# A four-layer graph network on one core: semaphores cleared inside blocks, scatters shared out anew, and products of constants where TensorE waits

## The reference

```python
edge_index = jnp.stack([src, dst])
x = _layernorm(x + _L0_gnn_ref(x, edge_index, W, b, a, 3125))
x = _layernorm(x + _L1_gnn_ref(x, edge_weight, W_lin, att_l, att_r, W_res, edge_index))
x = _layernorm(x + _L2_gnn_ref(x, edge_index, w_in, b_in, ...))
x = _layernorm(x + _L3_gnn_ref(x, weight, gamma, beta, src, dst, edge_type_8))
# layer 0, per head: num = segment_sum(exp(-lrelu(s_src[src] + s_dst[dst])) * h[dst], src); elu(num / row_sum)
# layer 1, 8 heads: softmax over dst of lrelu(edge_weight * (alpha_l[src] + alpha_r[dst])); sum of x[src]
# layer 2, two rounds: softmax over dst of q[dst].k[src] * scale; sum of v[src]; then w_o and a dense block
# layer 3: agg = segment_sum((h @ weight[rel])[src], dst); batch norm of agg
```

## Time and profile before

| | us |
|---|---|
| median of 3 runs (4961.72 to 4969.9) | 4966.9 |
| profiled execution, its own time | 4954.8 |
| its span, first to last instruction | 4953.0 |
| TensorE busy in the span | 3592.7 (73%) |
| DVE busy | 3404.9 (69%) |
| POOL busy | 2835.4 (57%) |
| ACT busy | 2076.2 (42%) |
| mean granted clock of TensorE | 0.854 of full speed |

### The profile page before, as it was taken

How to read it: one execution, slowest core, us unless ns; L and a number is a source line. 1 busy time by engine, 2 the same in 40 slices (tenths; PEclk the granted TensorE clock), 3 DMA queues, 4 the chain that set the end, 5 groups by cost and what they waited for, 6 DMA issues and landing times. The chain is left out here.

```text
span 4953.0 us, 58113 instructions
## 1 busy us (share of the span) xinstructions
PE 3592.7 (73%) x16423; PEld 2694.9 (54%) x16423; DVE 3404.9 (69%) x6660; ACT 2076.2 (42%) x4216; POOL 2835.4 (57%) x2961
## 2 busy tenths in 40 slices
PE   2455566654997887757888879978888799755553
PEld 1322455541456666634666658856666676444443
DVE  8876788866876666686999985579999642222225
ACT  1047444523873333244666644446666333100001
POOL 2775777757767777403777731057776210277772
PEclk9779777777997887878999989989999899877776
DMA  1100777762005554524888861178888321333334
GB/s 53 35 2 18 188 184 181 184 123 63 2 21 143 138 138 132 88 87 158 239 239 239 235 137 44 37 213 240 239 238 212 106 79 69 120 105 105 105 105 65
DMA packets 294343, 632.59 MB, mean 128 GB/s; under 512 B 70842, under 2 KB 149663, under 8 KB 290847
## 3 DMA queue, kind: packets, MB, share of 16 engines
q0 software_dynamic: 157120, 435.48, 33.7%
q1 hardware_dynamic: 136926, 193.54, 13.0%
HBM read 562.78 MB, written 66.02 MB: 127 GB/s over the span
## 5 line engine op out<-in xcount | busy, mean ns | idle before, releaser
L1046 PE MATMUL edge_sums<-edge_rows,edge_hot 128*128 128x272 f32 (+2 forms) x3712 | 1188.4, 482 | 643.4 <-issue 248.7
L1046 PEld LDWEIGHTS edge_sums<-edge_rows,edge_hot 128*128 128x128 f32 x3712 | 873.9, 243 | 884.7 <-issue 476.1
L980 POOL DMA_INDIRECT edge_rows<-kv_rows,dst_index x928 | 877.6, 946 | 574.5 <-POOLq L101 285.5
L980 POOL DMA_INDIRECT edge_rows<-rel_rows,dst_marks x464 | 438.7, 946 | 235.4 <-issue 137.1
L1056 DVE TENSOR_TENSOR l_acc<-l_acc,edge_sums 128x272 f32 (+2 forms) x928 | 394.5, 425 | 251.1 <-PE edge_sums L1046 202.1
L980 POOL DMA_INDIRECT begun_rows<-xl_rows,dst_index x464 | 443.4, 956 | 177.0 <-issue 135.9
L980 POOL DMA_INDIRECT edge_rows<-rows,src_index x464 | 438.7, 945 | 172.8 <-issue 161.1
L1311 PE MATMUL edge_own_rows<-dst_x,edge_hot_t 128*128 x1856 | 461.0, 393 | 32.0 <-ACT edge_hot_t L1010 22.3
L1311 PEld LDWEIGHTS edge_own_rows<-dst_x,edge_hot_t 128*128 128x128 f32 x1856 | 352.2, 195 | 93.2 <-issue 37.4
L1056 DVE TENSOR_TENSOR last_acc<-last_acc,edge_sums 128x256 f32 x232 | 97.7, 421 | 428.6 <-PE edge_sums L1046 428.4
L218 POOL DMA_INDIRECT table_src<-src_src_stage_all x257 | 273.1, 1062 | 177.6 <-POOLq L92 85.8
(11 more groups left out here) (472 smaller groups left out, 6973.7 us busy)
## 6 DMA issues: line engine op xcount, KB each, us to landing
edge_where<-local_dst SPq DMA_DIRECT2D x174, 256.0 KB, 3.6
rel_rows<-nodes_out SPq DMA_DIRECT2D x25, 1024.0 KB, 3.8
edge_where<-local_src SPq DMA_DIRECT2D x58, 256.0 KB, 3.6
edge_rows<-kv_rows,dst_index POOLq DMA_INDIRECT x928, 4.2
edge_lows<-low_dst SPq DMA_DIRECT2D x85, 156.2 KB, 5.9
kv_rows<-nodes_out SPq DMA_DIRECT2D x50, 260.0 KB, 2.0
edge_keys<-key_dst SPq DMA_DIRECT2D x85, 152.6 KB
edge_rows<-rows,src_index POOLq DMA_INDIRECT x464
```

Source lines behind the costliest of these rows:

```text
L980: pool.indirect_dma_start(out=self.rows[:, h * U + b, 0:self.width], out_offset=None, in_=self.source[:, :], in_offset=bass.IndirectOffset ...
L1046: last = nc.tensor.matmul(sums[p % len(sums)][:, 0:width], self.hot[s % 2][:, 2 * (p % 4) + i, :], self.half(s)[:, 2 * (p % 4) + i, first: ...
```

## The change

- `Phase.clear` and its barrier go. `Phase.sweep` clears the given-up semaphores in POOL's own sequence, at the head of "srcload", "dstload" and of the five edge passes.
- A `Scatter` has one set of `put` semaphores for its whole life, its ring is counted by column over all pieces, and only its last piece waits for all puts.
- The source table's share of one-hot products is 176 for 168; the base block has a piece of 11 for 20, "up0" 22 for 28. The rest of each table falls to the blends: 112 scatters for 111 in the source blend, 174 for 168 in the destination blend.
- `keep_busy` puts products of the identity and of ones into banks that are not in use: 16 before `project` waits for its weights, 24 at the head of "dstload", 10 in `flash_pass` before the last chunk's sums, 72 at the head of "nodes", and 36 at those of "nodes0" and "nodes1".

```diff
     def __exit__(self, *a):
         done = self.ctx.__exit__(*a)
         Phase.used += self.sems
-        if len(Phase.used) > 75:
-            Phase.clear(self.nc)
         return done
 
     @staticmethod
-    def clear(nc):
+    def sweep(nc):
         nc.clear_and_free_semaphores(Phase.used)
-        nc.all_engine_barrier()
         Phase.used = []
...
+def keep_busy(nc, k, bank, n):
+    for _ in range(n):
+        nc.tensor.matmul(bank[:, 0:P], k.ident[:, :], k.ones[:, :], start=True, stop=True)
...
         self.tag, self.table, self.next, self.share, self.fields = tag, table, 0, share, fields
+        self.put, self.sent = [hold.sem(f"{tag}_put{u}") for u in range(SLOTS)], [0] * SLOTS
...
-        put, sent = [ph.sem(f"{self.tag}_put{u}") for u in range(SLOTS)], [0] * SLOTS
-        for t in range(n):
-            u = t // LOOK % SLOTS
-            if t % LOOK == 0:
+        put, sent = self.put, self.sent
+        for at in range(self.next, self.next + n):
+            u = at // LOOK % SLOTS
+            if at % LOOK == 0:
                 after(pool, put[u], sent[u])
-            at = self.next + t
...
         self.next += n
-        for u in range(SLOTS):
-            after(pool, put[u], sent[u])
+        if self.next == ET - self.share:
+            for u in range(SLOTS):
+                pool.wait_ge(put[u], sent[u])
...
-            scatter_beside(nc, ph, block, (earlier, 20))
+            scatter_beside(nc, ph, block, (earlier, 11))
...
-        if stream is not None:
+        if stream is None:
             @block.gpsimd
             def _(pool):
+                Phase.sweep(nc)
+        else:
+            @block.gpsimd
+            def _(pool):
+                Phase.sweep(nc)
                 pool.wait_ge(indexed, 1)
                 stream.gather(nc, pool, None, 0, BEGUN)
...
         @block.tensor
         def _(pe):
+            if marks is not None:
+                keep_busy(nc, k, cut_bank, 24)
             pe.wait_ge(placed, 1)
...
         @block.gpsimd
         def _(pool):
+            Phase.sweep(nc)
             e.gather(nc, pool, summed, BEGUN if begun else 0)
...
                 if chunk(f):
                     expand(4 * f + 4)
+                tail(f)
                 if chunk(c):
                     pairs(2 * c, (0, 1, 2, 3))
+
+            def tail(f):
+                if f == CHUNKS:
+                    pe.wait_ge(multiplied, BATCHES if dot else HALVES)
+                    keep_busy(nc, k, own_rows[0][:, 0, :] if dot else own_rows[0], 10)
...
+            keep_busy(nc, k, prod[0], 16)
             pe.wait_ge(loaded, 16 * len(loads)) if loads else None
...
+            keep_busy(nc, k, down, 36 if own_merge else 72)
             if own_merge:
                 pe.wait_ge(have_a, have["a"])
...
-        attend_update(nc, k, "up0", acc, 2, x, 0, None, [(by_dst, 28)])
+        attend_update(nc, k, "up0", acc, 2, x, 0, None, [(by_dst, 22)])
...
-                    by_src = Scatter(near, "src", scratch("table_src", (TABLE, 4), i32), 168, 2)
+                    by_src = Scatter(near, "src", scratch("table_src", (TABLE, 4), i32), 176, 2)
```

More of the change, by code:

```diff
@@ L838, in load_order @@
             turned_at = lambda b: turned_p[0:size[b], b // 2, b % 2 * (P + 2):(b % 2 + 1) * (P + 2)]
-            cut_p = [ph.ps(f"cut_p{n}", [8, 512]) for n in range(2)]
+            cut_bank = ph.ps("cut_bank", [P, 512])
+            cut_p = [cut_bank[0:8, :], ph.ps("cut_p1", [8, 512])]
             keys_s = ph.sb("keys_s", [P, CHUNKS, P + 2])
```

## The result

The change took **4940.2 us** (median of 5 runs, 4938.8 to 4944.1) against 4966.9 before: 26.7 us less, a ratio of 0.9949 (95% interval 0.9936 to 0.9963). Timed again beside its variants it took 4938.0 against 4962.0, 0.9954 (0.9940 to 0.9968). 4936.8 had been forecast, in a range of 4919 to 4953. The total came out right; its parts did not all, and one sentence about the passes was false.

The account below looks back on a forecast made before the run. POOL's back-to-back gathers were taken to bound the edge passes, leaving block ends, pass tails and node-stage starts to gain. Terms summed to -30.1 us, subtracted from the 4966.9 median: 4936.8 us, range 4919 to 4953.

Parts of the forecast that it names:

- Scatters moved: Fewer scatters in base block (-12.4 us) and update (-8.5); more in source blend (+1.3) and destination blend (+2.3).
- The formula 2.4 + 0.08 x n: At block ends: POOL's idle time in us from its last scatter to the next block's first, after n scatters.
- rival 5: Moved scatters hit a slower blend: ACT passes POOL in the source blend, or POOL lags in the destination blend; 4946.8, chance 0.04.
- cover: Source blend: POOL ends after ACT, which would have to slow by over 2 us to take over.
- Waits for puts: Dropping the wait at a piece's end in both projections and two sort blocks: -0.5 us each, -2.0 in all.
- Clears: Semaphore clears: five barriers gone, -5.0 us; the clears at 0.65 each on the passes' path, +3.3; together -1.7.
- Fillers: Products of constants keeping TensorE's clock high: two third-layer tails -5.2 us, first later node stage -2.2, second -1.7, elsewhere 0.
- Projections and second loading stage: nothing. POOL ends all three: The 16, 16 and 24 products of constants there gain and cost nothing, since POOL is last in each block.
- Nothing of a pass but its tail depends on TensorE: Edge passes: POOL issues gathers back to back, 1.26 us each; only what follows its last gather hangs on TensorE.
- The page's rule: TensorE's clock: read as only a longer single gap between bursts losing full speed; first later node stage would then give -4.4.
- Rival 1: The clock is low again at TensorE's own work everywhere, despite products of constants; only -21.0 remains, 4945.9 us, chance 0.22.
- The seams: Block ends, pass tails and node-stage starts; without any gain from TensorE's clock, -21.0 us remains.

Follow-up runs that it names:

- The shares alone: Kernel before with only 11 scatters for 20 in the base block, 22 for 28 in the update, 176 columns for 168 in the source blend: 4944.5 us, ratio 0.9971.
- the puts alone: Kernel before with only put semaphores that last and no wait at the end of a piece but the last: 4947.2 us, ratio 0.9967.
- the clears alone: Kernel before with only the semaphore clearing moved into POOL's own blocks and no barrier after it: 4968.1 us, ratio 1.0009.

## Why the prediction was right, and where not

- **Scatters moved:** right, and to about a microsecond. Base -12.4 (forecast -12.4), update -8.0 by the shares and -9.0 with the waits gone (-8.5), source blend +0.7 to +2.6 (+1.3), destination blend +2.9 by the shares and +3.1 in the change (+2.3); together -16.8 alone for -17.3. POOL's lag and DVE's end were the right two things to compare. The formula 2.4 + 0.08 x n would have failed in the destination blend: it gives 16.3 for 174 scatters, and POOL ended that block 8.2 us after its last. The 7.3 taken instead, from 49 scatters, was near by luck. ACT never ended the source blend (rival 5), but its cover was down to 1.0 us in the change.
- **Waits for puts:** the mechanism was right, the size too small. The term "-0.5 each, -2.0 in all" measured 1.0 to 1.8 in each of the four blocks, 5.6 together; POOL's lag fell by 1.3 to 1.4 in all but one. The step that failed is the choice of row: I went by 16 gathers without such a wait, and a gather is not a scatter. The upper bound of 1.4 was the answer.
- **Clears:** the sum "-5.0 + 3.3" was nearly right, its two parts were not. The five stretches took 5.4 us. Ahead of the three passes that had one, the first gather comes within 0.3 us of where it came before, so the clear costs there what the stretch did, 1.1 and not 0.65; the first two passes, which had none, pay 0.2 and 0.3 for theirs. That leaves about -1.3 for -1.7.
- **A term that the sum lacks:** the first pass's first gather comes 2.0 us sooner than before in the change. The shares alone and the puts alone have it too (2.2 each), the clears alone have 1.3 the other way, and the profile shows no wait there. The cause is open.
- **Fillers:** "-5.2, -2.2, -1.7" measured about 0 in the sum. In the third layer's tails (from POOL's last gather to the pass's end) twelve without fillers average 46.7 us, sixteen with them 45.2: -1.5 each, for -2.6. The lower size has one reason in the rows: fillers at the falling clock took 3.43 us for 2.3. nodes0 averages 310.1 in the six traces without fillers and 308.9 in the eight with them, -1.2 for -2.2, with both kinds between 307 and 311.4. nodes1 averages 413.8 and 414.9: +1.1 for -1.7. Against these stands what the sentence "Projections and second loading stage: nothing. POOL ends all three" missed: POOL does end the stage, but in all four traces with the fillers one of its issues took 9.7 us beside DVE's comparisons, and that cost 7 us. I had asked which engine ends the block and not what the earlier engine would run into, though the update's rows of before have such issues.
- **"Nothing of a pass but its tail depends on TensorE"** was false for edge1. The earlier trace rows leave that pass out. Its gathers took 572 us for POOL's 563 already before, and up to 585 in other traces. That error cost the forecast nothing, as the change put no filler there, but it hid the largest gain, 19 to 22 us.
- **The page's rule** (Trainium skill, TensorE: Matmul & The Clock Gate, "Why this matters for your kernels") is to leave no longer gap between bursts; that only such a gap takes the clock back is drawn from it by the prediction, and not said there. What was drawn fails here a second time: in nodes, with the gap bridged, the clock fell after gaps of 0.38 to 1.40 us between own products. With bridged gaps and dense own work, in nodes0 and nodes1 of the same trace, it stayed.
- Rival 1 (4945.9, the clock's part worth nothing) had the better account of the fillers. The total was right because errors stood against each other, which is luck: fillers priced some 9 us too well; against that, waits for puts 3.6 us too low and the 2.0 us of the first pass not in the sum. The seams, forecast at -21.0, add up to about -26 in the rows of the change.

## What to carry to other kernels

An engine at 80% that alternates between two clocks can set the pace of a loop that another engine seems to bound; look at the window of the bound engine for its own pace (1.258 us an issue here) and ask what every slower stretch waits for. Products of constants paid measurably only inside that loop, in small numbers ahead of the waits at which the clock fell, and not in starts and ends. Before speeding up an engine off the path, name the engines that it will make collide, and look in the trace for issues that already lasted long beside them. Before trusting a difference of two traces, have the stage in two traces of the same kernel, and compare their time at the low clock.

## What the runs showed of the hardware that was not expected

- An indirect DMA's issue on POOL lasted 9.7 us beside 20 DVE comparisons of 0.55 us each, and 1.1 to 1.3 us beside the same ones in other executions; tiny instructions between them didn't matter, and where DVE paused in them even for 0.06 us no issue was long. Beside single DVE operations of 6.8 and 11.2 us issues took 6.5 and 11.0 us, in the kernel before too.
- Passes of the same instructions differ by 16 us (edge1, 620.6 to 636.8) from kernel to kernel and, judged by a spread of up to 17 us between runs of one kernel, probably from run to run. Their length follows the time that TensorE spent at the low clock, 253 to 293 us. With the fillers inside edge1 its five traces lie between 611.4 and 614.0, with 142 to 158 us at the low clock.
- POOL's idle time at a block's end grows by 0.07 to 0.08 us for each indirect DMA of that block from 13 to 59, with or without a wait for their landing. It doesn't go on so: after 174 it was 8.2 us.
